# Expert gates by a DVE transpose and a transfer through DRAM, and the expert pairs summed on GpSimd

## The reference

```python
x = x + attn(layernorm(x))                     # 16 heads of 64, causal
y = layernorm(x)
cont = sigmoid(y @ enc_W + enc_b) @ s2c_W + s2c_b              # (4096, 64)
logits = tanh(cont @ rW1 + rb1) @ rW2 + rb2                    # 8 experts
probs = softmax(logits); w, i = top_k(probs, 2); w = w / w.sum()
gates = (one_hot(i, 8) * w[..., None]).sum(1)                  # (4096, 8)
h = relu(einsum('nm,emh->enh', cont, We1) + be1)               # hidden 128
expert_out = einsum('enh,ehm->enm', h, We2) + be2              # 64 wide
output_flat = einsum('enm,ne->nm', expert_out, gates)
dec = sigmoid(sigmoid(output_flat @ c2s_W + c2s_b) @ dec_W + dec_b)
x = x + layernorm(dec) * ln_g + ln_b
```

## Time and profile before

| | |
|---|---|
| runs, us | 1211.62, 1206.49, 1210.98; median 1210.98 |
| profiled execution, us | 1213.07 |
| its span, us | 1211.4 |
| busy over the span, us | PE 1095.8, DVE 915.3, ACT 715.2, POOL 619.7 |
| mean granted clock of TensorE | 0.966 of full |

### The profile page before, as it was taken

The page is one execution under the profiler, slowest core; times in us unless marked ns, Lnnn a source line. Parts: engine busy times, 40 slices in busy tenths (PEclk is TensorE's granted clock), DMA queues, the critical chain, the costliest instruction groups (busy, mean ns, idle before and its releaser), DMA issues.

```text
span 1211.4 us, 51581 instructions
## 1 busy us (share of the span) xinstructions
PE 1095.8 (90%) x19964; PEld 777.8 (64%) x19964; DVE 915.3 (76%) x2231; ACT 715.2 (59%) x1497; POOL 619.7 (51%) x628
## 2 busy tenths in 40 slices
PE   3779999999999999999999999999999647999995
PEld 1556777777777767677777777776777434454542
DVE  7467888888888888788788888888888673575663
ACT  4555656566666666566656565656656342666663
POOL 4385555555666665656665666555555221023232
PEclk8889999999999999999999999999999868999997
DMA  6656777667777777767777777776767530000000
GB/s 154 173 141 150 174 168 172 162 160 165 176 172 172 167 176 164 160 161 163 168 166 169 173 170 168 174 171 164 170 160 164 137 71 19 1 10 17 9 9 27
DMA packets 121648, 165.07 MB, mean 136 GB/s; under 512 B 44304, under 2 KB 55568, under 8 KB 121616
## 3 DMA queue, kind: packets, MB, share of 16 engines
q1 hardware_dynamic: 121616, 164.67, 58.3%
HBM read 109.80 MB, written 21.23 MB: 108 GB/s over the span
## 4 chain that ended last, share of the span: by engine, by line
PE 70%; DVE 12%; DMA 5%; issue 5%; ACT 3%; SPq 2%; POOL 2%; DVEq 0%; ACTq 0%; POOLq 0%
PE ZB L602 25%; PE SPS L585 12%; PE SPS L586 9%; DVE PTZ L887 6%; PE ZB L570 5%; DMA XTB<-xt_scratch 5%; PE ZB L575 4%; DVE SSB L947 3%; PE ZB L764 3%; PE ZB L610 2%; PE SPS L756 2%; SPq L413 1%; PE ZB L748 1%; PE ZB L782 1%; PE SPS L721 1%
## 5 line engine op out<-in xcount | busy, mean ns | idle before, releaser
L947 DVE CUSTOM_DVE_ANT_0 SSB<-SPS,MASK 128x640 f32<-128x640 f32 (+7 forms) x512 | 373.0, 746 | 166.2 <-PE SPS L586 134.2
L585 PE MATMUL SPS<-KHP,QS 128*128 (+2 forms) x768 | 331.4, 436 | 25.7 <-DVE NM L947 24.9
L602 PE MATMUL ZB<-PTZ,VR 32*64 32x256 f32 (+2 forms) x16384 | 331.5, 297 | 23.4 <-DVE PTZ L887 18.3
L1237 ACT ACTIVATE PRL<-SSB,NM 128x640 f32<-128x640 f32 (+3 forms) x256 | 252.8, 988 | 163.3 <-DVE NM L947 99.7
L602 PEld LDWEIGHTS ZB<-PTZ,VR 32*64 32x64 f32 x16384 | 266.0, 132 | 78.9 <-issue 63.4
L458 POOL TENSOR_TENSOR X<-X,OT 128x512 f32 (+1 forms) x64 | 82.0, 1281 | 358.3 <-ACT OT L1247 349.8
L586 PE MATMUL SPS<-KLP,QS 128*128 (+2 forms) x768 | 261.4, 348 | 0.0
L887 DVE STREAM_TRANSPOSE PTZ<-PRL 128x640 f32<-128x640 f32 (+3 forms) x256 | 255.0, 1025 | 0.0
L585 PEld LDWEIGHTS SPS<-KHP,QS 128*128 128x128 f32 x768 | 145.4, 189 | 117.6 <-issue 54.8
L1237 ACT ACTIVATE PRS<-SSB,NM 128x128 f32<-128x128 f32 (+3 forms) x256 | 142.0, 555 | 116.7 <-DVE NM L947 116.5
L452 POOL TENSOR_TENSOR KLP<-RAW,KHP 64x512 fp32r<-64x512 f32 x128 | 164.0, 1281 | 21.4 <-ACT KHP L1323 11.3
(11 more groups left out here) (158 smaller groups left out, 1084.3 us busy)
## 6 DMA issues: line engine op xcount, KB each, us to landing
VR<-v_scratch SPq DMA_DIRECT2D x256, 256.0 KB, 5.5
KHP<-KHP SPq DMA_DIRECT2D x64, 256.0 KB, 3.2
KLP<-KLP SPq DMA_DIRECT2D x64, 256.0 KB, 3.9
XTB<-xt_scratch SPq DMA_DIRECT2D x64, 256.0 KB, 3.2
v_scratch<-V SPq DMA_DIRECT2D x32, 512.0 KB, 7.7
RSB<-rcp_scratch SPq DMA_DIRECT2D x64, 256.0 KB, 4.0
WQK<-in_W_q SPq DMA_DIRECT2D x33, 64.0 KB
WQK<-in_W_k SPq DMA_DIRECT2D x33, 64.0 KB
```

The lines of the kernel that those rows point to most:

```text
L585: pe.matmul(SP_[n % 2][:, c0:c0 + wc], q, kh[:, c0:c0 + wc], start=True, stop=False)
L602: last = pe.matmul(ZB[h * DH:(h + 1) * DH, i, kt * TR:QT * TR], VR[rows, j, kt, h * DH:(h + 1) * DH], turned_block(h, kt, j, rows), start= ...
L947: v.tensor_tensor_reduce(out=SSB[n % 2][:, 0:w], in0=SP_[n % 2][:, 0:w], in1=MASK[:, S - w:S], scale=1.0, scalar=BIG, op0=ALU.add, op1=ALU ...
L1237: act.activation(exps_of(n), SSB[n % 2][:, 0:w], ACT.Exp, bias=NM[:, col:col + 1], scale=-1.0, accum_out=L[:, col:col + 1]).then_inc(exp_d ...
```

## The change

The gates stay on one path: DVE normalizes them into GE, transposes GE in 32x32 blocks into GT, SP writes GT to DRAM (16 KB), waits for that, and reads it back with two transfers of 512 KB, each of which repeats the four even or the four odd gate rows over 64 partitions: GATES, 128 x 4 x 512, in two buffers over VR, which attention no longer needs. They are made a chunk ahead. The PE transposes, the float32r split and the spreading matmuls go.

The second layer is now taken ungated. Experts 2p and 2p+1 go to the two halves of a PSUM bank WB[p] (four uses of three banks). DVE adds the bias and multiplies by the gate in one operation for each pair (`dve_gate`, L1075 of the changed kernel). POOL adds the four pair tiles in three operations (`sum_pairs`) to O. The upper and lower 64 rows of O are summed by c2s, whose weights stand twice on the partitions, as before. The encoder, continuation, router, decoder and the output's steps keep their operations but stand elsewhere in the orders of PE, DVE and ACT. In chunk 0 ACT's square root for the last batch row's input norm moves in front of the encoder's tanh. On SP the gates' transfers for chunk c+1 stand in front of the store of chunk c-1.

```diff
+        gate_dram = nc.dram_tensor("gate_scratch", (2, E, CH), F32, kind="Internal").ap()
...
+        O = PRS[:, 0:CH]
...
-        H, GH, O, SMT = F[0:2], F[2:6], F[6], F[7:9]
+        H, OG, SMT = F[0:4], F[4:8], F[8:10]
+        GE, GT = (PRS[:, 2 * CH + 512 + i * TC * E:2 * CH + 512 + (i + 1) * TC * E] for i in range(2))
+        GATES = [VR[:, i * 2:i * 2 + 2, :, :].rearrange("p a t c -> p (a t c)").rearrange("p (e n) -> p e n", n=CH) for i in range(2)]
...
+        WB = [Z, GB[0], GB[1], Z]
...
+            def spread_gates(c, par):
+
+                sp.wait_ge(f_gt, c + 1)
+                sp.nop(nofuse=True)
+                sp.dma_start(gate_dram[par].rearrange("e (t i c) -> i (e t) c", t=TC, c=TR), GT).then_inc(f_written, DMA)
+                sp.wait_ge(f_written, c * DMA + DMA)
+                sp.nop(nofuse=True)
+                for h in range(2):
+                    sp.dma_start(GATES[par][h * M:(h + 1) * M],
+                                 gate_dram[par].rearrange("(p h) n -> h p n", h=2)[h].partition_broadcast(M)).then_inc(f_spread, DMA)
+            sp.wait_ge(pv_done, STEPS * QT)
+            spread_gates(0, 0)
+
+            def chunk(c, par, first, last):
+                if not last:
+                    if not first:
+                        sp.wait_ge(f_og, c * 4)
+                        sp.nop(nofuse=True)
+                    spread_gates(c + 1, 1 - par)
+                if not first:
+                    store(c - 1)
+            each_chunk(sp, chunk)
+            store(NC - 1)
...
+            def sum_pairs(c):
+
+                for i in (0, 2):
+                    gp.wait_ge(f_og, c * 4 + i + 2)
+                    gp.tensor_tensor(OG[i], OG[i], OG[i + 1], ALU.add).then_inc(f_pairs, 1)
+                gp.wait_ge(f_pairs, c * 2 + 2)
+                gp.tensor_tensor(O, OG[0], OG[2], ALU.add).then_inc(f_o, 1)
+
             def chunk(c, par, first, last):
+                if not first:
+                    sum_pairs(c - 1)
                 if not last:
                     norm_in((c + 2) % NC, c + 2)
                 if first:
...
                 else:
                     finish(c - 1)
             each_chunk(gp, chunk)
+            sum_pairs(NC - 1)
             finish(NC - 1)
...
         def pe_experts(pe, c, p):
 
-            pe.wait_ge(f_gh, c * E + 2 * p + 2)
-            if p == 0:
-                wait(pe, f_o, c)
-            for e in (2 * p, 2 * p + 1):
-                last = pe.matmul(Z[(e % 2) * M:(e % 2 + 1) * M, :], W2[:, e, :], GH[e % 4], start=(p == 0), stop=(e == E - 1))
-            if p == E // 2 - 1:
-                for be2 in (BE2H, BE2L):
-                    last = pe.matmul(Z[0:M, :], be2[0:2 * LOW], GSTACK[0:2 * LOW], start=False, stop=be2 is BE2L)
+            pe.wait_ge(f_relu, c * E + 2 * p + 2)
+            wait(pe, f_og, c * 4 + (0, -2, -1, 1)[p])
+            for h in range(2):
+                last = pe.matmul(WB[p][h * M:(h + 1) * M, :], W2[:, 2 * p + h, :], H[(2 * p + h) % 4], start=True, stop=True)
             last.then_inc(f_w2, 1)
...
+            pe.wait_ge(out_copied, STEPS * 2)
+
             def chunk(c, par, first, last):
-                for e in (0, 1):
-                    pe_hidden(pe, c, par, e)
+                pe_hidden(pe, c, par, 0)
+                pe_hidden(pe, c, par, 1)
+                if not last:
+                    pe_encode(pe, c + 1)
+                pe_hidden(pe, c, par, 2)
+                pe_experts(pe, c, 0)
+                pe_hidden(pe, c, par, 3)
                 if not first:
                     pe_c2s(pe, c - 1, 0)
-                pe_gate_turn(pe, c)
-                if not last:
-                    pe_encode(pe, c + 1)
-                if first:
-                    pe.wait_ge(f_spread, 1)
-                    pe.wait_ge(out_copied, STEPS * 2)
-                else:
+                pe_hidden(pe, c, par, 4)
+                if not last:
+                    pe_cont(pe, c + 1)
+                if not first:
                     pe_c2s(pe, c - 1, 1)
-                for e in (0, 1):
-                    pe_gates(pe, c, e)
-                for e in (2, 3):
-                    pe_hidden(pe, c, par, e)
-                if not last:
-                    pe_cont(pe, c + 1)
-                for e in (2, 3):
-                    pe_gates(pe, c, e)
-                pe_experts(pe, c, 0)
+                pe_experts(pe, c, 1)
+                pe_hidden(pe, c, par, 5)
+                if not last:
+                    pe_router(pe, c + 1, 1 - par)
+                pe_hidden(pe, c, par, 6)
                 if not first:
                     pe_decode(pe, c - 1)
-                for e in (4, 5):
-                    pe_hidden(pe, c, par, e)
-                if not last:
-                    pe_router(pe, c + 1, 1 - par)
-                for e in (4, 5):
-                    pe_gates(pe, c, e)
-                pe_experts(pe, c, 1)
                 if not last:
                     pe_logits(pe, c + 1)
-                for e in (6, 7):
-                    pe_hidden(pe, c, par, e)
-                for e in (6, 7):
-                    pe_gates(pe, c, e)
                 pe_experts(pe, c, 2)
+                pe_hidden(pe, c, par, 7)
                 if not last:
                     pe_norm_turn(pe, c + 2)
                 pe_experts(pe, c, 3)
...
+            step(v.tensor_tensor(GE.rearrange("p (e t) -> p t e", t=TC), G1, over(RG), ALU.mult), 12)
+            wait(v, f_written, c * DMA)
+            v.transpose(GT, GE).then_inc(f_gt, 1)
...
+        def dve_gate(v, c, par, p):
+
+            v.wait_ge(f_w2, c * 4 + p + 1)
+            if p == 0:
+                v.wait_ge(f_spread, c * (2 * DMA) + 2 * DMA)
+                wait(v, f_o, c)
+            v.nop(nofuse=True)
+            v.scalar_tensor_tensor(OG[p], WB[p], BE2[:, p:p + 1], GATES[par][:, p, :], ALU.add, ALU.mult).then_inc(f_og, 1)
...
-                dve_gates_low(v, c)
-                for e in range(4):
-                    dve_gate(v, c, e)
-                if not last:
-                    dve_low(v, c + 1, 1 - par)
-                if not first:
-                    dve_decoded(v, c - 1)
-                dve_gate(v, c, 4)
-                dve_gate(v, c, 5)
                 if first:
                     v.wait_ge(out_evac, STEPS * 2 + 1)
                     f_norm_stats(v, range(NT - QT, NT))
-                else:
+                    f_norm_scale(v, 1)
+                if not last:
+                    dve_low(v, c + 1, 1 - par)
+                dve_gate(v, c, par, 0)
+                dve_gate(v, c, par, 1)
+                if not first:
+                    dve_decoded(v, c - 1)
+                if not last:
+                    gates_1(v, c + 1)
+                dve_gate(v, c, par, 2)
+                if not first:
                     dve_out_stats(v, c - 1)
                 if not last:
-                    gates_1(v, c + 1)
-                    gates_2(v, c + 1, {1: lambda: dve_gate(v, c, 6), 2: lambda: dve_gate(v, c, 7)})
-                else:
-                    dve_gate(v, c, 6)
-                    dve_gate(v, c, 7)
-                if first:
-                    f_norm_scale(v, 1)
-                else:
+                    gates_2(v, c + 1, {})
+                if not first:
                     dve_out_norm(v, c - 1)
+                dve_gate(v, c, par, 3)
...
+                wait(act, f_w2, c * 4 + e // 2 - 1)
+                act.activation(H[e % 4], TB[e % 2][:, :], ACT.Relu, bias=BE1[:, e:e + 1]).then_inc(f_relu, 1)
...
                 hidden(c, 0)
                 hidden(c, 1)
-                if not first:
-                    out_hidden(c - 1, 0)
-                gates_high(c)
+                if first:
+                    f_deviations(act, 1)
                 if not last:
                     encoded(c + 1)
...
```

More of the change, by code:

```diff
@@ L48 @@
 EPS = 1e-5
-GSTEPS = 14
+GSTEPS = 15
 DMA = 16
@@ L421, in store @@
                 sp.wait_ge(f_out, c + 1)
+                sp.nop(nofuse=True)
                 sp.dma_start(out_tiles[:, bass.ds(c * TC, TC), :], OUT).then_inc(stored, DMA)
-            with sp.Fori(0, NC) as c:
-                store(c)
+            def spread_gates(c, par):
[13 more added lines that the diff above has]
+                        sp.wait_ge(f_og, c * 4)
+                        sp.nop(nofuse=True)
+                    spread_gates(c + 1, 1 - par)
[3 more added lines that the diff above has]
+            store(NC - 1)
             sp.wait_ge(stored, NC * DMA)
@@ L734, in pe_logits @@
             last.then_inc(f_lg, 1)
[L736 to L742, removed]
         def pe_hidden(pe, c, par, e):
@@ L1015, in dve_step @@
             stats(8)
-            if last:
-                v.memset(GP, 0.0).then_inc(zeroed, 1)
             mask(14)
@@ L1061, in gates_2 @@
             step(v.reciprocal(RG, GS), 11)
-            wait(v, f_gt, c)
-            v.tensor_tensor(twice(GP), G1.unsqueeze(2).broadcast_to([P, TC, 2, E]),
```

(46 more changed lines are left out.)

38 lines of the change are left out of this document (9 added, 29 removed).

## The result

The changed kernel takes 1282.79 us at the median of 4 runs (1279.35 to 1287.42), the kernel before 1209.76 us (1206.49 to 1211.62) on the same chip: ratio 1.059, 95% interval 1.054 to 1.064, slower by 73 us. The forecast was 1292, in a range of 1264 to 1318. The profiled execution took 1280.16 us for a span of 1278.4.

The account below looks back on a forecast made before the run. PE bound the kernel before; a new loop through POOL's finish and store wait would bind after. O(0) at 1045.8, loops of 30.0, five of 34.0 and 26.5, tail 20: span 1292.3, median 1292 us, range 1264 to 1318.

Parts of the forecast that it names:

- PE remains the bound: Rival in the chunks: POOL's wait ends early, O(c) meets PE at c2s, chunks take 17 us, total 1180; chance 0.06.
- The clock stays full: Rival on PE's clock: no half rate after the gaps, six loops of 30.0 us, median 1265; chance 0.13.
- store and clock both late: Rival: late store landing and half rate also over decode, logits and pair 2; five loops of 38, some 1316; chance 0.17.
- O(0): Chunk 0's summed POOL output, ready at 1045.8 us, with 2.0 us saved on DVE ahead of the chunks.
- The first loop: From O(0) to O(1): 30.0 us at full clock, since PE is busy up to it.
- Middle loops: Five loops from O(1) to O(6): 34.0 us each, with the first 9 us at half clock.
- The walk to the norm: From O ready through PE's c2s and decode to the end of DVE's output norm: 22.05 us at half clock.
- POOL's part: From DVE's norm through finish, store wait (POOL free at 7.8) and three adds (4.0) to O(c): 11.9 us.
- The last loop: From O(6) to O(7), without next chunk or gate transfers: norm at 15.3, then 7.2 and 4.0, 26.5 us.
- The tail: From O(7) to the end: 20 us with c2s and decode at half rate, 16.2 us before.
- The spread: The gates' DRAM write and read-back: lands 5 to 9 us after the norm, not holding DVE's first gate operation.
- PE's own work: PE in a steady chunk loses spreading and bias matmuls, gate transposes and a detour: some 4.5 of 21.46 us.

Follow-up runs that it names:

- the last two kernels: "sums first" with DVE's pairs 0 and 1 ahead of the low-half subtraction, 4 us slower; the second adds pair 3 before the norm, 24 us slower than the version of 1202 us.
- the version of 1202 us: "sums first" with DVE's pair 3 moved ahead of the output norm, statistics still ahead of the gate chain; ratio 0.995 to the kernel before.
- the first kernel with the chain early: "sums first" with DVE's next-chunk gate chain ahead of the output's statistics and norm, pair 3 inside the chain; 26 to 28 us slower than "sums first".
- sums first: Changed kernel with POOL reordered to norm_in, the pair sums of chunk c, then finish(c-1); 1216 us, 66 us less than the changed kernel.

## Why the prediction was right, step by step

The mechanism was the forecast's, and its loop was read off the traces of before: the sums behind finish and the store, c2s behind the sums, half clock behind the gap. The rival "PE remains the bound" (1180) needed POOL 10 us sooner; of the kernels that sum ahead of finish the best reached 1202. "The clock stays full" and "store and clock both late" failed on the rows above. The sum of 1292.3 against a span of 1278.4 is 13.9 us too high, nearly all of it in these terms. The medians are only 9 apart, which is luck: I took the median 2.1 us below the profiled execution, and it came out 2.6 above it.

- *O(0)*: 1045.8 forecast, 1042.6 measured. POOL's last operation of attention starts 4.7 us earlier than in the trace of before, where I took 2.0 for the work ahead of the chunks. I do not lay that on the change: in the traces of the experiments, with the same attention, it starts anywhere from 1007.5 to 1020.6. So single traces are compared here by their loops and not by their spans.
- *The first loop*: 30.0 and 30.3. Its full clock was right.
- *Middle loops*: 34.0 each; 32.5, 32.9, 33.7, 31.8, 33.3, so 5.7 us too many in all (and from norm to norm 32.1 to 33.5, where I had said 33 to 35). Two terms were off, with opposite signs. The walk to the norm was 22.05 and is 20.0 (1105.4 to 1125.4), because the half rate ended by 1111, within 6 us, and not 9 us after work resumed: decode starts 9.1 us after O, not 10.85. I had carried over the length of the earlier trace rows unchanged; the earlier trace rows also had 0.53 over 7 us only, and I took the longer. POOL's part is 12.9 and not 11.9: free 9.1 us after the norm (forecast 7.8), sums 3.8 (forecast 4.0). The 9.1 lies inside my 7 to 10; I chose nearly the idle rate although the read-back stood in front of the store. A part of the middle loops' closeness is thus luck: 2.0 us too many in the walk, 1.0 too few on POOL.
- *The last loop*: 26.5 and 23.6, of which some 2 us are in the walk, where the half rate ends earlier, and 0.7 in POOL's way from the norm to the sums, 6.5 us where I took 7.2. *The tail*: 20 and 17.6; half rate, 0.78 over 7.2 us behind O(7), is there too shorter than I took it.
- *Bias and gate in one operation*: 0.70 and 0.75. *The spread*: 5 to 9 us after the norm, measured about 7 to 8; DVE waits for it once, 1.7 us, in the changed kernel. Costing it at nothing held because pair 0 stands behind a longer wait of DVE, 19.57 us for the continuation (L1066) in the chunk above; the last two kernels show it without that cover.
- *PE's own work*: 4.5 us less in the forecast; 17.72 us busy in the first loop, at full clock, against 21.39, so 3.7 less.

Where the 73 us come from, by kernels: 66 go with POOL's order. Inside these, 30 go with the store's wait alone, and of the 30 a part, 11, with the read-back ahead of the store. The half clock's 2.3 us a loop lie inside the 66 too. The 7 that remain, and 7 more, go once pair 3 also stands ahead of the norm.

## What to carry to other kernels

When an operation moves to a helper engine, walk that engine's program order first: everything ahead of the new operation, its waits for transfers too, joins the path. A sum that the next stage waits for belongs ahead of a finish that nobody waits for; and moving one operation in one queue needs a look at each other queue where its reader stands ahead of something urgent (the root on ACT). Price a transfer by what stands in its queue at that moment.

## What the runs showed of the hardware

Some of DVE's operations stretch while POOL runs its adds. In the version of 1202 us the norm's four operations take 3.17 us beside POOL's pair sums, 1.11 in the changed kernel; one of them 1425 ns at the most against 340. In the first kernel with the chain early, operations on two SBUF operands (L1051, L1052, 128x256) take 1.37 us each, in "sums first" 0.42 and 0.43. The two engines in the version of 1202 us:

```profile
1103.23 1.28 POOL L564 TENSOR_TENSOR PTZ<-PTZ 128x512 f32<-128x512 f32 x1 [5.66 <-DVE PTZ L1073]
...
1103.28 3.17 DVE L1094 TENSOR_SCALAR SSB<-PTZ,MV,RS 128x128 f32<-128x128 f32 x4
```

The Trainium skill, page GPSIMD Engine Reference, section 1. Specifications, has POOL's interfaces to SBUF shared with VectorE. The traces agree, and show that here it is DVE that gives way: POOL's adds keep their 1.27 us. Not every operation of DVE is hit: beside POOL's adds L1073 and L1075, which read one operand from PSUM, kept 0.75 us, and two statistics beside L564 (L1082), which read one tile of SBUF, their 0.28 us each.

The granted clock came back sooner than in the two places of before, and not always after the same time. Two stretches of the changed kernel that begin about where c2s does:

```profile
1073.00:1080.00 7.00, 7.00 (x15) 3.04 (x16) 0.80 (x2) 3.22 (x5) 1.94 (x2) 0.76 0.00 1
...
1138.00:1145.00 7.00, 6.61 (x10) 3.06 (x10) 0.00 (x0) 1.62 (x3) 2.38 (x3) 0.53 0.00 0
```

With two levels, 0.76 over 7 us is 3.4 us at 1.2 GHz and the rest at 2.4, and 0.53 is 6.6 us, of which 0.4 lie ahead of c2s. Worked out in this way for the five middle loops, PE ran at 1.2 GHz for 3.4, 5.0, 6.2, 3.2 and 5.5 us after gaps of 9.6 to 10.7 us, and the loops took 32.5, 32.9, 33.7, 31.8 and 33.3 us: the longer the half clock, the longer the loop (POOL's wait for the store varies by 0.4 us beside it).
